# TensorE's transposes of a tile's GRU result at the end of their half step, behind the count groups

## The reference, cut to what matters

```python
h = layernorm(x)                                    # x: 6250 nodes x 256
msg = h[src] + relvectors[edge_type]                # 200000 edges, sorted by dst
red = segment_sum(msg, dst)                         # per node
gi, gh = red @ w_ih.T + b_ih, h @ w_hh.T + b_hh     # GRU cell
r = sigmoid(i_r + h_r); z = sigmoid(i_z + h_z); n = tanh(i_n + r * h_n)
x = x + (1 - z) * n + z * h
h2 = layernorm(x)
mask = the best 2 of 8 experts by h2 @ Wg + bg
x = x + sum over chosen experts of gelu(h2 @ W1 + b1) @ W2 + b2
```

## Time and profile before

| | us |
|---|---|
| median of 3 runs | 1563.23 (1562.03 to 1563.25) |
| the profiled execution, its own time | 1562.57 |
| its span, first to last instruction | 1560.7 |
| PE busy | 1292.3 (83%) |
| DVE busy | 1013.0 (65%) |
| POOL busy | 993.0 (64%) |
| ACT busy | 732.4 (47%) |

### The profile page before, as it was taken

How to read it: one execution, slowest core, us unless ns; L and a number is a source line. 1 busy time by engine, 2 the same in 40 slices (tenths; PEclk the granted TensorE clock), 3 DMA queues, 4 the chain that set the end, 5 groups by cost and what they waited for, 6 DMA issues and landing times. The chain is left out here.

```text
span 1560.7 us, 36074 instructions
## 1 busy us (share of the span) xinstructions
PE 1292.3 (83%) x12887; PEld 1056.9 (68%) x12887; DVE 1013.0 (65%) x2768; ACT 732.4 (47%) x1489; POOL 993.0 (64%) x868
## 2 busy tenths in 40 slices
PE   1269998999999999998899998775572999999991
PEld 1145566777777777777777777665562899999990
DVE  7857765576677777777878886864344555555550
ACT  6424453555455555554334342322131767676660
POOL 2077764676667777777777777777732455555551
PEclk9659998999999999999999999887675999999996
DMA  9686632444444555454544543443933466555556
GB/s 292 177 208 188 182 89 84 140 135 127 132 121 134 141 138 148 132 146 119 142 129 133 140 134 109 116 125 115 328 82 96 70 96 96 94 95 91 96 79 185
DMA packets 132379, 209.99 MB, mean 135 GB/s; under 512 B 26552, under 2 KB 99837, under 8 KB 130919
## 3 DMA queue, kind: packets, MB, share of 16 engines
q0 software_dynamic: 60032, 112.63, 30.7%
q1 hardware_dynamic: 72167, 94.97, 20.9%
HBM read 158.70 MB, written 57.76 MB: 139 GB/s over the span
## 5 line engine op out<-in xcount | busy, mean ns | idle before, releaser
L716 POOL DMA_INDIRECT ring<-h_table,idx x648 | 680.4, 1050 | 296.0 <-issue 211.3
L1728 PE MATMUL P<-hs,amat 128*126 128x512 f16 (+4 forms) x1568 | 403.6, 391 | 0.0
L833 ACT ACTIVATE amat<-P 128x300 f16<-128x300 f32 (+4 forms) x440 | 175.9, 445 | 253.7 <-PE P L1715 252.2
L770 POOL DMA_INDIRECT out_rows<-yo,xrows x112 | 177.0, 1580 | 162.2 <-DVE yo L1592 110.0
L1728 PEld LDWEIGHTS P<-hs,amat 128*126 128x126 f16 (+4 forms) x1568 | 182.4, 130 | 92.9 <-issue 7.8
L1710 PE MATMUL P<-cone,lone 128*128 128x294 f16 (+4 forms) x920 | 182.0, 294 | 44.7 <-ACT amat L833 39.0
L725 POOL DMA_INDIRECT expert_rows<-xrow,slots x100 | 126.3, 1263 | 67.9 <-DVE slots L1335 38.1
L1583 DVE SCALAR_TENSOR_TENSOR gl<-gT,scales,gh 128x512 f16<-128x512 f32 x112 | 84.2, 752 | 127.7 <-ACT gh L960 127.7
L1192 DVE TENSOR_TENSOR cone<-src_t,twice 128x1176 f16<-128x1176 f16 (+4 forms) x230 | 164.4, 715 | 0.0
L1942 PE MATMUL P<-xh,w_all 128*128 128x256 f16 x896 | 157.8, 275 | 0.0
L1955 PE MATMUL P<-w_all,gh 128*128 x896 | 149.8, 273 | 0.7 <-DVE gl L1583 0.7
(11 more groups left out here) (244 smaller groups left out, 2751.4 us busy)
## 6 DMA issues: line engine op xcount, KB each, us to landing
raw<-in_L_ffn_W_dram SPq DMA_DIRECT2D x32, 512.0 KB
xrows<-expert_rows SPq DMA_DIRECT2D x56, 257.0 KB, 3.1
ring<-h_table,idx POOLq DMA_INDIRECT x648
w_parts<-parts SPq DMA_DIRECT2D x16, 512.0 KB
w_all<-w_parts SPq DMA_DIRECT2D x8, 1024.0 KB, 20.2
h_in<-h_table SPq DMA_DIRECT2D x25, 250.0 KB
x<-in_x_dram SPq DMA_DIRECT2D x25, 250.0 KB
out_rows<-x SPq DMA_DIRECT2D x25, 250.0 KB
```

Source lines behind the costliest of these rows:

```text
L716: nc.gpsimd.indirect_dma_start(out=ring[:, r, j, :], out_offset=None, in_=h_dram, in_offset=bass.IndirectOffsetOnAxis(ap=idx[:, slot, g * ...
L770: nc.gpsimd.indirect_dma_start(out=out_dram, out_offset=bass.IndirectOffsetOnAxis(ap=xrows[:, b % XR, j, D:D + 1].bitcast(I32), axis=0), i ...
L833: nc.scalar.activation(amat[:, b % 2, :, s * aw:(s + 1) * aw], bank[:, 0:HIS * aw].rearrange("p (h w) -> p h w", w=aw), ACT.Copy).then_inc ...
L1728: nc.tensor.matmul(both, amat[:, b % 2, hi, 0:used], hs[:, hi, :], start=(hi == 0), stop=False)
```

## The change

The loop over the tiles at stage 6 moves, in TensorE's order of a half step, from ahead of the first burst to behind the last burst and piece. In half steps of stage 6 that have count groups (tiles 0 to 19) the transposes are so moved past the first burst, `sums`, and all pieces and bursts. Tile 20 (half step 144) has no count groups, but `sums` and a piece. In the half steps of tiles 21 to 24 none of these is issued. No other engine's order changes, and nothing is added or removed.

```diff
                     for i in stage_of(h, 0):
                         transpose_h(i)
-                    for i in stage_of(h, 6):
-                        transpose_gru(i)
                     if bursts:
                         head_burst(bursts[0])
                     if s == 0 and n < NS:
...
                         if m + 1 < len(bursts):
                             head_burst(bursts[m + 1])
+                    for i in stage_of(h, 6):
+                        transpose_gru(i)
                     for i in stage_of(h, 1):
                         gate_hn(i)
```

## The result

Six runs of each kernel: 1568.15 us after (1565.85 to 1570.15), 1562.22 before (1558.48 to 1563.25), a ratio of 1.0043 [1.0022, 1.0064]. The change makes the kernel slower by 6 to 7 us. The profiled execution of after is the lowest of its six, 1565.85 us, with a span of 1564.0.

The account below looks back on a forecast made before the run. POOL follows TensorE until about 850 us, so the end moves by what TensorE has lost by then: 10.4 + 0.6 = 11 us, taken as 8, on 1562.57 gives 1570.6; forecast 1570.5, range 1559 to 1580.

Parts of the forecast that it names:

- The mechanism: DVE's residual waits for TensorE's half step; ACT's root, count moves, `low_h` and raw weights queue behind; tile 2 loses 1.1 us.
- the tiles that were named: Tiles 0 to 9, where the late residual was to lose 10.4 us in all.
- prediction's terms: Loss worked out tile by tile: 10.4 us in tiles 0 to 9, 0.6 in 10 to 14, 0 behind 850 us.
- tiles 10 to 13: DVE is late there, so part of TensorE's removed wait is kept: 0.7, 0.2, 0 and 2 us, 2.9 together.
- tile 14's 3.5: Transposes wait behind the row of `cone`; the residual moves to about 820.7, raw load and ACT behind it: 3.5 us lost.
- Tile 0's 3.1: The first raw load hangs on DVE's second norm behind the residual, TensorE on ACT behind that load: whole 3.1 us lost.
- the raw term: Tile 8: ACT waited 0.75 us for raw weights, whose issue moves 1.5 us later: 1.4 us lost.
- The discount: Some losses fall into waits already there, as POOL's 37 us early show: 8 us taken of 11.
- One sign: POOL's real waits from 200 to 526 us up by about 8, the last gather later by as much as the whole.
- From there on its own pace: From about 850 us POOL runs at its own pace to the last gather, last tiles following unchanged; TensorE's gains there: 0.
- The clock: Faster rival: low clock behind the transposes' wait goes, at most 3.3 us at tile 13; 1557 us; both faster rivals 0.13 together.
- The faster rival: The wait was the bound: TensorE keeps what it no longer waits, up to 11 us, 1552; both faster rivals 0.13 together.

Follow-up runs that it names:

- Experiment 4: Against the kernel before: three of four transposes stay ahead, the fourth goes to the end of the half step and releases the residual; 1580.17 us, ratio 1.0140.
- experiment 5: The change, with ACT's root moved behind its half step's count moves, against the kernel before: 1563.24 us, ratio 1.0021.
- experiment 1: Against the kernel before: the transposes at the end of their half step in tiles 0 to 9 alone; 1570.8 us, ratio 1.0066.
- 2: Against the kernel before: the transposes at the end of their half step in tiles 10 to 20 alone; 1560.13 us, ratio 1.0003.
- experiment 7: Kernel before, with transpose_h's matmuls written ten times more: early, in tiles 4 and 6, 1566.28 us, ratio 1.0053; late, in tiles 17 and 18, 1554.87 us, ratio 0.9988.
- experiment 6: Raw weight loads moved ahead of SP's wait for the residual: on top of the change 1564.66 us, ratio 1.0041; on the kernel before 1558.78 us, 0.9991.
- Experiment 8: Against before: transposes behind first burst and `sums`, 1554.67 us, 0.9974; with raw loads early too, 1551.83 us, 0.9950; with the root last as well, 1553.47 us, 0.9966.
- experiment 3: Kernel before, with a TensorE no-op at the end of the half step releasing the residual: 1563.18 us, ratio 1.0017.

## Why the prediction was right, and where not

It forecast 1570.5 us, 0.47% over the median of before, and gave slower a chance of 0.67; measured are 0.43% and 1568.15 us. Its last step slipped: 1570.6 for the profiled execution and 0.7 for the median make 1571.3, not 1570.5. Nothing hangs on that.

*The mechanism* held at each step: the wait off TensorE, onto the residual, the root behind the variance instead of behind its table load, the count moves behind the root. Experiment 4 shows the new wait alone as dear, 5 shows that half of the loss or more goes by the root, 1 and 2 show it in the tiles that were named.

*The terms, tile by tile.* How much later a tile's first transposes (`transpose_h`) start than before measures all that was lost up to the second tile ahead of it. Tile 0 starts 0.4 us earlier in the profile of after, so 0.4 is added to each shift read there (the shifts quoted for the experiments are less their own tile 0's in the same way):

```
lost through tile    0    1    2    4    6    8    9   11   13   14
prediction's terms  3.1  3.9  5.0  4.4  8.3  9.7 10.4  9.5  7.5 11.0
measured            2.0  3.4  5.6  3.2  9.2  9.7 11.0  9.1  6.4  6.2
```

One execution each, and still the first ten tiles come to 11.0 where 10.4 were worked out (11.2 in experiment 1's first kernel, 12.2 in experiment 4), and tiles 10 to 13 give back 4.6 where 2.9 were. How far single cells can be trusted is seen in the late kernel of experiment 7, which is that of before up to 850 us and ought to read 0: it reads -1.7 through tile 0, 1.9, 0.6 and -1.3 through tiles 12, 13 and 14, and within 0.4 in the others.

*The failed term is tile 14's 3.5.* The row of `cone` and the late residual came as told (3.28 and 4.38 us of wait), but "with the raw load and ACT behind it" did not: between 815 and 859 us ACT has no wait for raw weights at all, and TensorE's two waits for count moves there sum to 2.4 us against 1.9 before. From the start of tile 15's first transposes to that of tile 16's, in before, after and the late kernel of experiment 7 (columns as in the earlier trace rows):

```profile
809.74:852.64 42.90, 38.93 (x391) 31.13 (x390) 34.08 (x98) 16.62 (x39) 31.02 (x27) 0.88 0.44 126
...
815.73:858.43 42.70, 36.98 (x391) 29.13 (x390) 34.03 (x98) 16.42 (x39) 31.86 (x29) 0.92 0.48 133
...
810.96:851.92 40.96, 37.41 (x390) 29.60 (x389) 34.09 (x98) 16.52 (x39) 31.53 (x28) 0.92 0.48 135
```

TensorE idles 5.72 us of it after and 3.97 before, so the term is some 1.7, half of what was told. That the table has nothing for it comes of the granted clock: 0.88 in the profile of before, 0.92 in the other two, and the same matmuls take 1.95 us less after.

*Tile 0's 3.1* was charged whole to the first raw load. The table has 2.0, in two waits, of which before had 4.97 us for the second and none for the first:

```profile
226.66 0.48 PE L1710 MATMUL P<-cone,lone 128*128 128x343 f16 x2 [0.96 <-ACT amat L833]
...
245.14 0.47 PE L1710 MATMUL P<-cone,lone 128*128 128x343 f16 x1 [6.09 <-ACT amat L833]
```

The first stands behind the root and is not there in experiment 5; the second, 1.1 us longer, stands behind ACT's wait for the first raw weights (6.2 us, 5.1 before). So the path was right for half of it. For tile 8 the profile of experiment 6 bears out the raw term: there the shift falls by 0.5 us where the change's rises by 0.9, the 1.4 of the sum.

*The discount* from 11 to 8 was put down to losses that fall into waits of POOL. Up to 850 us the sum is 6.2 after all, but not by such waits: tiles 10 to 13 gave back 1.7 more than told, and tile 14 reads 3.7 less, of which the clock of one execution is about 2. That the 8 came near the measured 6 to 7 is luck in part.

*One sign did not come.* POOL's real waits from 200 to 526 us were to rise by about 8 and rose by 1 (by 4.5 up to 850). The window is fixed in time: POOL issues 177 gathers in it where it issued 180, so what is lost shows in gathers that are still to come and not in longer waits. The other half of the sign, the last gather later by as much as the loss, did come (7.5 us).

*"From there on its own pace"* is right as to TensorE's gains (experiment 7, late) and wrong as to what follows: the last tiles did not go on unchanged behind the last gather. It is 7.5 us later, the last scatter 3.5; in the profile of experiment 5 these are 5.3 and 1.2, in that of 6 3.6 and 3.7. The scatter keeps to the start of tile 24 each time (later by 4.0, 1.3 and 3.9 us); what lets this tile start less late than the last gather is open.

*The clock* as a rival: tile 13's stretch at half clock did vanish, and tile 13 kept 2.9 us where 2 were taken; another came at 507.5 us, between tiles 7 and 8, where tile 6's loss falls: 4.7 us where 2.6 were worked out. Both go with the order in all fourteen profiles: from 503 to 520 us the granted clock is 0.80 or 0.90 in the five kernels that release tile 6's residual by a matmul at the end of the half step and 1.00 in the other nine, and from 768 to 792 us it is 1.00 in the seven that move tile 13's transposes whole, to the end or in between, and 0.86 or 0.93 in the other seven. In sum it does not explain the loss: from 200 to 850 us half clock was granted for 37 us in both profiles, before and after (mean clock 0.97). No experiment holds it still, so its share of a single tile is not shown. The Trainium skill (TensorE: Matmul & The Clock Gate, Part 1) has the low clock as the default that activity lifts; the trace agrees in so far as the new stretch stands behind a new wait.

*The faster rival* was wrong for this change and right in one thing: the removed wait is worth time. Experiment 8 gets it by moving the transposes half as far.

## What to carry to other kernels

A wait that is removed by issuing a producer later moves to whatever consumes it: price the queue behind the consumer, on its engine and on the next ones, before the wait itself is counted as gain. Work out such a chain half step by half step from one timeline each, and ask up to which point in time the engine that sets the end still follows. And try the positions between "first" and "last": here the one in the middle takes more than half of the wait off one engine and puts little of it on the other.

## What the runs showed of the hardware

- A no-op in TensorE's order that updates a semaphore does so while matmuls ahead of it in the order are still to begin: 17 of them in tile 8, the last of which ended 2.9 us later (experiment 3). The residual waited 10.9 us for it in six tiles, and 51.2 in twenty-one for a transpose in the same place (experiment 4).
- An indirect DMA of POOL at its own pace is mostly 0.95 to 1.25 us busy and 0.30 us not. So an engine at "78 of 100" can be full: from 900 to 1000 us of the trace of before its 71 instructions make 78.4 us busy, and with 0.3 us for each 99.7; and 8.5 us more of TensorE's work beside it cost nothing (experiment 7).
- The table load ahead of ACT's root takes 1.28 us, and the root can follow 0.01 us behind it.
- A stretch of half clock can come and go with a wait of TensorE: one at 771 us went with the wait ahead of the transposes, and one at 507.5 us came with a wait of 2.59 us for ACT.
